# A four-layer graph kernel on one core: its pipeline cut from groups of eight graphs to halves of four

## What is computed

```python
x = ln(x + GAT4(x, adj))        # 4 heads: softmax over neighbours, elu
x = ln(x + GRU3(x, adj))        # 3 rounds: aggr = A^T (h W_i); h = gru(aggr, h)
x = ln(x + REL(x, adj))         # sum over relations r of (adj == r) x W_r, + bias
x = ln(x + GAT1(x, adj))        # 1 head, 256 features, elu

def gru(m, h):                  # applied to each node
    r, z = sigmoid(Wir m + Whr h + b), sigmoid(Wiz m + Whz h + b)
    n = tanh(Win m + bin + r * (Whn h + bhn))
    return (1 - z) * n + z * h
```

## Time and profile before

| | us |
|---|---|
| median of 3 runs | 2903.97 (2903.3 to 2910.07) |
| profiled execution, its own time | 2902.69 |
| its span, first to last instruction | 2900.5 |
| PE busy in the span | 2708.2 (93%) |
| DVE, ACT, POOL busy | 2175.1, 1648.5, 1307.8 |

### The profile page before, as it was taken

One profiled execution on the slowest core, in us unless ns is written; L12 is line 12 of the kernel. 1 busy time (PEld: TensorE's weight loads), 2 busy tenths in 40 slices (PEclk: granted clock), 3 DMA queues, 4 the chain that ended last, 5 costly groups with the idle time before them and its releaser, 6 DMA issues. The chain is left out here.

```text
span 2900.5 us, 48930 instructions
## 1 busy us (share of the span) xinstructions
PE 2708.2 (93%) x15577; PEld 2321.7 (80%) x15577; DVE 2175.1 (75%) x5170; ACT 1648.5 (57%) x4164; POOL 1307.8 (45%) x1351
## 2 busy tenths in 40 slices
PE   4589999999999999999999999999999999999944
PEld 2478888888888888888888888888888888888833
DVE  6467778787877878787887878787787878787643
ACT  0445566665666566566656656566666656664422
POOL 0033545444455545445454544445454444545422
PEclk8589999999999999999999999999999999999976
DMA  6000000000000000000000000000000000000000
GB/s 192 19 21 15 21 25 21 23 25 19 23 28 21 28 16 25 26 26 19 25 25 25 20 25 25 17 25 29 21 22 22 25 23 23 25 21 10 10 12 15
DMA packets 97279, 75.31 MB, mean 26 GB/s; under 512 B 6625, under 2 KB 92769, under 8 KB 96993
## 3 DMA queue, kind: packets, MB, share of 16 engines
q1 hardware_dynamic: 77296, 54.28, 6.5%
q10 hardware_dynamic: 19696, 17.44, 1.8%
HBM read 54.93 MB, written 16.78 MB: 25 GB/s over the span
## 5 line engine op out<-in xcount | busy, mean ns | idle before, releaser
L928 PE MATMUL psum<-ag_h,wc_h 128*128 128x512 f32 x1152 | 482.9, 419 | 0.3 <-DVE ag_l L1269 0.3
L928 PE MATMUL psum<-ht_h,whh_h 128*128 128x512 f32 x1152 | 472.7, 410 | 0.0
L928 PE MATMUL psum<-ht_h,whh_l 128*128 128x512 f32 x1152 | 456.6, 396 | 0.0
L928 PE MATMUL psum<-ag_l,wc_h 128*128 128x512 f32 x1152 | 456.3, 396 | 0.0
L928 PE MATMUL psum<-ht_l,whh_h 128*128 128x512 f32 x1152 | 455.2, 395 | 0.0
L928 PE MATMUL psum<-ag_h,wc_l 128*128 128x512 f32 x1152 | 454.2, 394 | 0.0
L1344 POOL TENSOR_SCALAR rstd<-moments 128x2 f32<-128x2 f32 x256 | 95.0, 371 | 743.3 <-DVE moments L1181 742.1
L1398 POOL TENSOR_TENSOR ht<-ht,g_n 128x512 f32<-128x512 f32 x192 | 258.3, 1345 | 271.2 <-ACT g_n L1089 268.0
L1393 POOL TENSOR_TENSOR ht_l<-ht,ht_h 128x1024 fp32r<-128x1024 f32 x64 | 153.9, 2404 | 290.6 <-DVE ht_h L1295 290.6
L928 PEld LDWEIGHTS psum<-ht_h,whh_l 128*128 128x128 f32 x1152 | 216.7, 188 | 52.3
L928 PEld LDWEIGHTS psum<-ag_h,wc_l 128*128 128x128 f32 x1152 | 216.3, 188 | 51.9
(11 more groups left out here) (151 smaller groups left out, 7178.9 us busy)
## 6 DMA issues: line engine op xcount, KB each, us to landing
adj_i<-in_adj_dram SPq DMA_DIRECT2D x128, 128.0 KB, 2.1
x_in<-in_x_dram SPq DMA_DIRECT2D x64, 256.0 KB, 2.8
out_dram<-out_t ACTq DMA_DIRECT2D x64, 256.0 KB, 2.1
adj_g<-in_adj_dram SPq DMA_DIRECT2D x32, 256.0 KB, 3.3
hh_raw<-in_L_gnn_w_hh_dram SPq DMA_DIRECT2D x1, 768.0 KB, 7.3
ih_raw<-in_L_gnn_w_ih_dram SPq DMA_DIRECT2D x1, 768.0 KB, 10.9
wl_raw<-in_L_gnn_weight_dram SPq DMA_DIRECT2D x1, 768.0 KB, 12.4
wrs<-in_L_gnn_weight_dram SPq DMA_DIRECT2D x1, 768.0 KB, 10.1
```

Source lines behind the costliest of these rows:

```text
L928: last = mm(dst, s, m, start=(first and k == 0), stop=(last_part and k == len(flat) - 1))
```

## The change

The list of steps is now one table, `HALF`, run for t = -2 to 34 with the steps that fall outside the 32 halves left out. In a pass t the GRU layers 0 and 1 of half t stand around layer 2 of the half ahead (`gru_agg(-1,2,0)` and what follows). A pass holds two `pre` units (unit 1 of half t+1, and the beginning of unit 0 of half t+2) and the two `post` units of half t-2, whose relational part begins in the pass before. The operations of each engine are the same but for one: x1 lives in three buffers (`x1[k % 3]`), the residual is read from there, and the copy to `x1r` is gone. `x3` has two buffers. Semaphores that counted several things are split (`s_ht0_l`, `s_nd0_l`), since halves no longer pass them in the order of the counts.

```diff
-         "post_pen": 2, ... "x2s": 1, "h1": 1, "mt": 1, "adjt": 1, "x3": 1,
+         "post_pen": 2, ... "x2s": 1, "h1": 1, "mt": 1, "adjt": 1, "x3": 2,
...
+         "adjg": 1, "nodes": 1, "agg": 1, "adjf": 1, "out": 1, "yr": 1, "yf": 1, "x1": 3}
...
-TRIP = """
-gru_agg(0,0,0)  next.pre_load(0)  last.post_load(0)  next.att_xt(pre,0)
...
+HALF = """
+post_load(-2,1)  rel_split(-2,1)  rel_y1(-2,0)  rel_rest(-2,0)
+gru_agg(0,0,1)  gru_new(-1,1,0)  att_scores(pre,1,0,0)
...
+def placed(step, t, halves):
+    name, a = step[0], step[1:]
+    kind, a = (a[:1], a[1:]) if name.startswith("att") else ((), a)
+    k = t + a[0]
+    if not 0 <= k < halves:
+        return []
+    if name.startswith("gru"):
+        return [(name, k) + a[1:]]
+    return [(name,) + kind + (2 * k + a[1],) + a[2:]]
+
+def program_order(halves):
+    return [s for t in range(-2, halves + 3) for step in half_steps(HALF) for s in placed(step, t, halves)]
...
-        x1n = [sb(f"x1n{b}", [P, 4, D]) for b in range(2)]
-        x1r = [sb(f"x1r{b}", [P, 4, D]) for b in range(2)]
+        x1 = [sb(f"x1{i}", [P, 4, D]) for i in range(SLOTS["x1"])]
...
-                nc.vector.tensor_copy(x1r[b][:], x1n[b][:]).then_inc(s_x1r, 1)
...
-                dve.wait_ge(s_x1r, nth(v, step, 2, b))
-                tt(y_t[yi][:], ..., x1r[b][:, 2 * hf:2 * hf + 2, :], ALU.add).then_inc(s_fin_y, 1)
+                tt(y_t[yi][:], ..., x1[k % 3][:, 2 * hf:2 * hf + 2, :], ALU.add).then_inc(s_fin_y, 1)
```

More of the change, by code:

```diff
@@ L172 @@
-gru_r(0,0,1)  last.att_xt(post,0)
-gru_z(0,0,1)  last.post_load(1)
-gru_in(0,0,1)  next.pre_load(1)  gru_new(0,0,0)  next.att_pt(pre,0,1)
-gru_agg(1,0,0)  last.att_wh(post,0,0)  gru_n(0,0,1)
-gru_agg(1,0,1)  last.rel_split(1)
-gru_hn(1,0,0)
-gru_rzh(1,0,0)  last.att_wh(post,0,1)  last.rel_adjt(1)
-gru_r(1,0,0)  last.att_scores(post,0,0)  gru_new(0,0,1)  last.rel_mask(1)  next.att_pv(pre,0)  last.gru_norm(1,1)
-gru_z(1,0,0)  last.att_prob(post,0)  last.post_load(2)  next.att_xt(pre,1)  next.att_exp(pre,0)  gru_split(0,0)
@@ L181 @@
-gru_in(1,0,0)  last.rel_h1(1)
-gru_hn(1,0,1)  next.att_res(pre,0)  last.att_pt(post,0,0)  gru_n(1,0,0)
-gru_rzh(1,0,1)  last.att_pv(post,0)  last.rel_y1(1)
-gru_r(1,0,1)  last.att_exp(post,0)  gru_new(1,0,0)  gru_turn(0,0,0)  gru_turn(0,0,1)  last.att_res(post,0)
-gru_z(1,0,1)  last.rel_rest(1)  next.att_wh(pre,1,0)
-gru_in(1,0,1)
-gru_agg(0,1,0)  next.att_norm(pre,0)  gru_n(1,0,1)
-gru_agg(0,1,1)
-gru_hn(0,1,0)
-gru_rzh(0,1,0)  last.att_norm(post,0)  next.att_wh(pre,1,1)  next.att_scores(pre,1,0)
@@ L200 @@
-gru_agg(1,1,0)  next.att_xt(pre,2)  gru_n(0,1,1)
-gru_agg(1,1,1)  gru_new(0,1,1)  next.att_exp(pre,1)  gru_split(0,1)
-gru_hn(1,1,0)
-gru_rzh(1,1,0)  last.post_load(3)  last.att_prob(post,1)  last.rel_h1(2)  last.att_pt(post,1,0)
-gru_r(1,1,0)  last.att_pv(post,1)  last.rel_y1(2)  last.att_exp(post,1)  last.att_res(post,1)  next.att_res(pre,1)
-gru_z(1,1,0)  next.att_wh(pre,2,0)  last.rel_rest(2)
-gru_in(1,1,0)  last.att_norm(post,1)
-gru_hn(1,1,1)  gru_turn(0,1,0)  gru_n(1,1,0)  gru_turn(0,1,1)  last.rel_norm(2)
@@ L232 @@
-gru_in(1,2,0)  next.att_res(pre,3)  last.att_pt(post,3,0)  next.gru_turn0(0,0)  next.gru_turn0(0,1)  gru_n(1,2,0)
-        last.att_pv(post,3)  gru_new(1,2,0)
-gru_hn(1,2,1)
-gru_rzh(1,2,1)  last.att_exp(post,3)  gru_norm(0,1)  last.att_res(post,3)
-gru_r(1,2,1)
-gru_z(1,2,1)  gru_n(1,2,1)
-gru_in(1,2,1)  next.att_norm(pre,3)  last.att_norm(post,3)  last.att_store(post,3)  gru_new(1,2,1)
+    if name == "att_norm" and a[0] == "pre" and a[1] % 2 == 0:
+        out.append("x1")
+    return out
+HALF = """
@@ new lines @@
+gru_r(-1,2,0)
+gru_z(-1,2,0)  att_res(post,-2,0)  att_pt(pre,1,1,0)  gru_n(-1,2,0)  gru_split(0,0)
+gru_in(-1,2,0)
+gru_hn(-1,2,1)  att_pt(pre,1,1,1)  att_wh(post,-2,1,0)  gru_turn(0,0,0)
+gru_rzh(-1,2,1)  gru_turn(0,0,1)  att_wh(post,-2,1,1)  att_pv(pre,1,1)  gru_new(-1,2,0)  att_xt(pre,2,0)
+gru_r(-1,2,1)  att_exp(pre,1,1)
+gru_z(-1,2,1)  att_res(pre,1,1)
+gru_in(-1,2,1)  att_scores(post,-2,1,0)
+gru_agg(0,1,0)  gru_n(-1,2,1)
+gru_agg(0,1,1)  att_prob(post,-2,1)
+gru_hn(0,1,0)
+gru_rzh(0,1,0)  att_wh(pre,2,0,0)  gru_new(-1,2,1)  gru_fin(-1,0)  att_pt(post,-2,1,0)
@@ L239, with half_steps @@
+gru_r(0,1,0)  att_norm(pre,1,1)
+gru_z(0,1,0)  gru_nodes0(1)  att_pv(post,-2,1)  gru_fin(-1,1)
+gru_in(0,1,0)  gru_norm(-1,0)  rel_split(-1,0)  rel_adjt(-1,0)
+gru_hn(0,1,1)  att_exp(post,-2,1)  att_wh(pre,2,0,1)  rel_mask(-1,0)  att_norm(post,-2,0)  gru_turn0(1,0)
+gru_rzh(0,1,1)  gru_n(0,1,0)  att_res(post,-2,1)  gru_turn0(1,1)
+gru_r(0,1,1)
+gru_z(0,1,1)  rel_h1(-1,0)
+gru_in(0,1,1)  gru_norm(-1,1)
+gru_agg(1,0,0)
 """
-def trip(first, last):
+def half_steps(text):
     steps = []
-    for word in TRIP.split():
+    for word in text.split():
@@ L265, in number_uses @@
[L265 to L280 removed]
+        steps.append((name,) + tuple(a if a in ("pre", "post") else int(a) for a in args.split(",")))
@@ L781, in _ @@
+            sp.wait_ge(s_out, 16 * 2 * HALVES)
         @block.tensor
```

851 lines of the change are left out of this document (361 added, 490 removed).

## The result

| | before | after |
|---|---|---|
| median | 2903.64 (2902.59 to 2910.07, 4 runs) | 2814.3 (2813.75 to 2819.75, 4 runs) |
| span of the profiled execution | 2900.5 | 2811.9 |
| PE busy | 2708.2 (93%) | 2686.6 (96%) |

The ratio is 0.9692 (95% interval 0.9674 to 0.9711): 89 us less, where 63 were forecast (2841). 2814.3 is the very edge of the prediction's range for 8 in 10 (2814 to 2875), and it lies under the range that the prediction gave its own sum (2816 to 2865).

The account below looks back on a forecast made before the run. PE bounds the middle; the question was its surroundings. Setup 66.6 + work 2630 + start 36 + first passes 12 + middle 30 + end 67 = 2842, by passes 2837; span taken 2838, median 2841, 8-in-10 range 2814 to 2875.

Parts of the forecast that it names:

- The 2630 us of work: Whole kernel behind the setup: 16 full trips of 164.4 us of PE work, unchanged since the matmuls stay the same.
- Start, gain 28: Before the first neighbour sum: two units ahead instead of four, sum at 115, 36 us of nothing instead of 64.
- First pass, 10 to 11 lost: First pass: 6.3 us gap before layer 1's first `gru_agg` plus about 4 of lower clock; the first trip lost 6.
- Copy costed at nothing: DVE's copy to `x1r`, 22.4 us in all, goes away; by itself this gives nothing on PE.
- Middle, 1.0 us of waiting a pass: Some 30 full passes: PE waits 1.0 us each, 30 in all against 27 before; bounds 0.3 and 4.4 a pass.
- End, gain 40: Last half's layer 2 and last units: 104 us, 66 of nothing plus 1 in the pass before, against 107.
- The 17.2: Between the last two units: distance 17.2 us instead of 24.2, because x3 has two buffers; bounds 12.8 and 24.2.
- The 42 us up to the final turn: Layer 2 of the last half beside half 30's `post` units: 42 us for 28 of work, its operand late.
- The slower rival: `gru_fin` waits for `gru_new`: slower from 3.1 us of waiting a pass, DVE 4 us later; 2943 at the bound; 1 in 12.
- The *better* rival: Start and end shortened by more, middle without waits: 0.3 a pass, end cadence 13; 2816 and less; 1 in 12.
- The gap and the clock: First pass: by the skill, the 6.3 us gap lowers PE's clock and would cost another 4 or so.
- DVE beside POOL: The 2.55 us cast stands 5 us behind `hn_l`; if together, DVE 2 us later, PE 9 to spare, sum unchanged.

Follow-up runs that it names:

- start4: The changed kernel with the first-layer steps of units 2 and 3 put back ahead of the first node sum; 2847.81 us, ratio 0.9801 to the kernel before.
- the tuned kernel: The changed kernel with steps of its last and first passes reordered, the middle untouched; 2820.6 us, ratio 0.9711 to the kernel before.
- end4: The changed kernel with the last GRU steps all ahead of the last two halves' post steps, undoing their overlap; 2839.27 us, ratio 0.9779 to the kernel before.

## Why the prediction was right, point by point

- **Direction and structure**: right. The 2630 us of work stayed, and what changed was what surrounds it, at the places named.
- **Start, gain 28**: right. The sum stands at 115.4, where 115 was forecast; undoing this part costs 33.5 us, 3.7 of them because start4's sum is later than that of the kernel before.
- **First pass, 10 to 11 lost**: right in size (60.9 for 61), but that it came so close is partly luck, since the same pass took 66.6 us in other executions (below), and wrong in place. The wait of 5.4 stands at `att_pt` of the second unit, for its exponent, not ahead of the first `gru_agg` of layer 1. The turn's own chain is as late, as the tuned kernel showed.
- **Copy costed at nothing**: right for the kernel before (ratio 1.0001), and not contradicted for the changed kernel: the 9 us there are the price of 1.9 us of copies a half, while the old copy's 0.70 would fit into idle time of DVE (an estimate).
- **Middle, 1.0 us of waiting a pass**: the mis-sized term, and nearly the whole miss. It measured 0.33 (9.0 / 27). The count behind it was right: it had found 0.3 a pass and 1 us in hand at `gru_fin` (measured 1.3); the 1.0 was then taken because the old trip had it. 0.67 x 29 is 19 of the 27 us missed. With 0.3 the prediction's own sum gives 2841 - 0.7 x 30 = 2820, not the 2816 at which its range began. The wait stands at `rel_y1`, for the low part of h1, a place that the prediction did not name, and by which it said it would be wrong: it had costed what stands ahead of `gru_fin` and `att_pt`, not DVE's queue between the turn of x1 and h1. Of the other 8, 1 is the short last pass, and the rest is PE work: 82.0 a pass without waits, where 82.2 was carried over. That 0.2 is spread over many steps, and its cause stays open.
- **End, gain 40**: right in size (178.9 us from the last half's first neighbour sum on, where 72 + 104 = 176 were forecast), right for the two units that moved beside layer 2 (25 by end4, some 17 without its break between the halves), wrong in cause for the distance of the units. The 17.2 measured 16.8, but it came with the order of the steps on PE, DVE and ACT (22 us by the end's order alone, with one x3 buffer); in the new order the second buffer is worth 0.6. That a chain costed for another reason gave 17.2 is luck in part. The 42 us up to the final turn came out too, but its stated parts, 15 + 20 + 4.4, add to 39.4.
- **The slower rival**: its place and mechanism are real. It was said to need DVE 4 us later and 3.1 us of waiting; 3.4 us later and 2.0 of waiting were enough to be level with the kernel before (ratio 1.0019), since in two passes of three the clock fell too. The *better* rival, 0.3 a pass, is what the middle did, with 64 us at the end and not less.
- **The gap and the clock**: the prediction's own sum left out what a gap costs in clock, and the first pass came out at 60.9 with 0.89. The clock did fall behind the gap (0.50 from 149 to 152 us, 1.00 from 155 on). The next section shows the same gaps with 5.7 us more. By the Trainium skill, TensorE: Matmul & The Clock Gate, section HAM oscillation, the prediction had reckoned about 4 there. The runs agree with it in part: the lower level stands behind the gap each time, but how long it stays differs, so that the profiled execution of the changed kernel paid some 2 us (an estimate: PE worked about 4 us at the lower level, from 149.1 to 153), and others 5.7 more.
- **DVE beside POOL**: the prediction had the cast of `ht_h` (128x512) clear of `hn_l` on POOL, and 9 us to spare for PE behind it. It is clear of `hn_l`, but the first of the two casts in a pass meets POOL's `x<-x,bias_rel` instead and takes 1.50 us for 0.40. And the cast is the head of the chain to h1's low part, the one place of the middle where PE waits: this is the step that the prediction did not follow.

## What to carry to other kernels

Where a pipeline's fill and drain leave the bound engine idle, cut the stage, and price it by what stands ahead of the first and behind the last full pass: that came out within 3 us. In the middle, count the slack of each wait and test it by adding work to the engine that is late; a count should not be overruled by the old kernel's average. A distance between units is set by several queues one behind another, and taking one away shows only the next, so price the chain with all of them moved before a buffer is named as the cause. And before a wait is taken away, look at what the step that is moved covers where it stands.
